# Norms of queries and keys by logarithm and exponential, and x centred and turned ahead of the bias layer's steps

## The reference

```python
xn = ln(x, g_norm)
q = (xn @ Wq).reshape(b, n, HEADS, DIM_HEAD).transpose(0, 2, 1, 3)
kv = xn @ Wkv
k, v = (kv[..., :DIM_HEAD], kv[..., DIM_HEAD:])
q = l2norm(q) * q_scale
k = l2norm(k) * k_scale
sim = jnp.einsum('bhid,bjd->bhij', q, k) * SCALE
bias = rel_pos_bias(n, w0, b0, g0, w1, b1, g1, w2, b2, q.dtype)
...
attn = jax.nn.softmax(sim, axis=-1)
out = jnp.einsum('bhij,bjd->bhid', attn, v)
...
def rel_pos_bias(n, w0, b0, g0, w1, b1, g1, w2, b2, dtype):
    pos = jnp.arange(-n + 1, n, dtype=dtype)[:, None]
    h = jax.nn.silu(ln(pos @ w0 + b0, g0))
    h = jax.nn.silu(ln(h @ w1 + b1, g1))
    h = h @ w2 + b2
```

## Time and profile before

| what | value |
|---|---|
| median of 3 runs (lowest to highest) | 252.21 us (251.5 to 252.31) |
| the profiled execution's own time | 251.66 us |
| its span | 249.9 us |
| busy: TensorE, VectorE, ScalarE, GpSimd | 210.8, 162.8, 122.1, 58.4 us |

### The profile page before, as it was taken

One profiled execution on the slowest core, in us unless ns is written; L12 is line 12 of the kernel. 1 busy time (PEld: TensorE's weight loads), 2 busy tenths in 40 slices (PEclk: granted clock), 3 DMA queues, 4 the chain that ended last, 5 costly groups with the idle time before them and its releaser, 6 DMA issues.

```text
span 249.9 us, 4768 instructions
## 1 busy us (share of the span) xinstructions
PE 210.8 (84%) x1906; PEld 141.4 (57%) x1906; DVE 162.8 (65%) x360; ACT 122.1 (49%) x178; POOL 58.4 (23%) x75
## 2 busy tenths in 40 slices
PE   0188798478897899999979989997889999999992
PEld 0154364343453464547356655764556899999992
DVE  2888779819148386889858975973953745474424
ACT  0216497677364255371634347538666542553230
POOL 3605949990000001200410027020003012000000
PEclk9999999999999999999999999999999999999997
DMA  6910055000003503400530070000000000000000
GB/s 187 422 44 0 0 146 199 4 1 0 3 0 63 129 3 107 84 0 3 116 77 0 24 155 16 0 3 0 3 3 1 4 0 21 3 21 0 21 0 21
DMA packets 10068, 11.75 MB, mean 47 GB/s; under 512 B 928, under 2 KB 9648, under 8 KB 9792
## 3 DMA queue, kind: packets, MB, share of 16 engines
q1 hardware_dynamic: 10048, 11.47, 16.5%
HBM read 10.38 MB, written 1.09 MB: 46 GB/s over the span
## 4 chain that ended last, share of the span: by engine, by line
PE 52%; DVE 27%; ACT 8%; POOL 5%; issue 4%; DMA 2%; DVEq 0%; SPq 0%; ACTq 0%
PE banks L1671 13%; PE banks L1376 6%; PE banks L1730 5%; DVE probs L958 5%; PE banks L1343 4%; PE banks L1271 3%; PE banks L1478 3%; PE banks L1396 2%; PE banks L1419 2%; PE banks L1438 2%; DMA rows<-in_rows 2%; ACT probs L594 2%; DVE zin L975 2%; ACT probs L556 2%; PE banks L1404 2%
## 5 line engine op out<-in xcount | busy, mean ns | idle before, releaser
L958 DVE TENSOR_TENSOR probs<-probs,eb 128x1024 f32<-128x1024 f32 x24 | 28.7, 1209 | 17.9 <-ACT probs L556 17.9
L594 ACT ACTIVATE probs<-banks,shift 128x1024 f32<-128x1024 f32 x24 | 25.9, 1112 | 14.9 <-PE banks L1461 14.7
L556 ACT ACTIVATE probs<-banks,key_shift 128x1024 f32<-128x1024 f32 x24 | 25.9, 1112 | 12.0 <-PE banks L1343 11.5
L1343 PE MATMUL banks<-qt,kT 64*128 64x512 f32 x96 | 25.4, 628 | 2.6 <-ACT probs L556 2.1
L1376 PE MATMUL banks<-probs,kvt 128*64 128x512 f32 (+1 forms) x128 | 23.3, 496 | 3.7 <-DVE probs L958 3.4
L363 POOL TENSOR_TENSOR qin<-qss,minus_half 128x16 f32<-128x16 f32 x8 | 23.1, 2903 | 6.4 <-DVE qss L797 6.3
L356 POOL TENSOR_TENSOR ve<-mv,ln_eps 128x2 f32<-128x2 f32 x4 | 1.7, 428 | 82.6 <-DVE mv L985 82.6
L1376 PEld LDWEIGHTS banks<-probs,kvt 128*64 128x64 f32 x128 | 7.8, 137 | 16.9 <-issue 9.7
L1671 PE MATMUL banks<-keys_space,wb 128*128 128x256 f32 (+1 forms) x72 | 17.3, 381 | 0.0
L1271 PE MATMUL banks<-wa,on 128*128 128x512 f32 x32 | 16.1, 628 | 1.2 <-DVE spread L803 1.2
L1203 DVE SCALAR_TENSOR_TENSOR x<-banks,ga,x 128x96 f32<-128x96 f32 (+1 forms) x32 | 10.2, 318 | 10.2 <-PE banks L1730 7.4
(11 more groups left out here) (214 smaller groups left out, 424.2 us busy)
## 6 DMA issues: line engine op xcount, KB each, us to landing
spread<-softmax_inverse_sums SPq DMA_DIRECT2D x16, 256.0 KB, 5.9
eb<-bias_table SPq DMA_DIRECT2D x4, 512.0 KB, 5.9
wb<-in_wb SPq DMA_DIRECT2D x1, 1842.0 KB, 10.5
wa<-in_wa SPq DMA_DIRECT2D x1, 1160.0 KB, 7.0
x<-in_x SPq DMA_DIRECT2D x1, 512.0 KB, 3.8
softmax_inverse_sums<-zin SPq DMA_DIRECT2D x4, 128.0 KB, 1.7
out<-x SPq DMA_DIRECT2D x4, 128.0 KB, 1.8
rows<-in_rows SPq DMA_DIRECT2D x1, 456.0 KB, 5.6
```

What stands on the lines that cost most here:

```text
L556: nc_.activation(pb[c], sc[:, 1024 * (c % 2):1024 * (c % 2 + 1)], ACT.Exp, bias=key_shift[:, b, k:k + 1]).then_inc(s["exp_done"], 1)
L594: nc_.activation(pb[c], sc[:, 1024 * SLOT[c]:1024 * (SLOT[c] + 1)], ACT.Exp, bias=shift2[:, 3:4]).then_inc(s["exp2_done"], 1)
L958: v.tensor_tensor(p, p, w, ALU.mult).then_inc(s["mult_done"], 1)
L1343: last = mm(out.rearrange("p (m i) -> p m i", m=rhs.shape[1]), lhs, rhs, start=True, stop=True)
```

## The change

- On ScalarE and GpSimd: the inverse roots of query tiles 3 to 7 and of the keys are no longer a power on GpSimd, or a square root on ScalarE with a reciprocal on VectorE, but exp(-0.5 ln) on ScalarE and one Newton step of four small instructions on GpSimd. Tiles 0 to 2 keep the power. The two loads of function tables in the stage are replaced by one, of a set that holds logarithm and exponential, between the last keys' copy and their turned copy.
- The keys are turned unscaled: GpSimd writes them twice side by side (`keys_doubled`), and their inverse length is applied as the scale of the exponentials of the first attention. `keys_out` moves from ScalarE to VectorE.
- The order at the end of the stage: two of the key turns go ahead of `turn_queries(5)`, two behind the first scores, which wait for the first sequence's keys alone; `queries_out(7)` stands behind the first exponential.
- In the front both halves of x have their statistics and the centring of the first half ahead of `bias_first`; the copies of the turned halves stand ahead of `bias_norm` and `bias_silu`; on TensorE keys and values of sequence 0 and queries 0 stand ahead of the turn of the bias rows and their product.

```diff
@@ gpsimd
+            def newton(ss, root, once, done):
+                def then(ins):
+                    steps[0] += 1
+                    ins.then_inc(s["root_step"], 1)
+                    pool.wait_ge(s["root_step"], steps[0])
+                then(pool.tensor_tensor(once, root, root, ALU.mult))
+                then(pool.tensor_tensor(once, once, ss, ALU.mult))
+                then(pool.tensor_scalar(once, once, -0.5, 1.5, ALU.mult, ALU.add))
+                pool.tensor_tensor(root, root, once, ALU.mult).then_inc(s[done], 1)
+            def query_newton(t):
+                pool.wait_ge(s["query_roots"], t - 2)
+                pool.wait_ge(s["qinv_ready"], t)
+                newton(qss[:, t], qin[:, t], q_once[:], "qinv_ready")
+            def key_newton():
+                pool.wait_ge(s["key_roots"], 1)
+                newton(kss[:], kin[:], ksr[:], "kinv_ready")
+            def keys_doubled():
+                pool.wait_ge(s["kvt_ready"], B)
+                pool.tensor_copy(kn, kvt[:].rearrange("p b t c -> p (b t) c")[:, :, None, 0:DH].to_broadcast([P, 3 * B, 2, DH])).then_inc(s["kn_ready"], 1)
...
             rstd(mv_x[:, 0:4, 1], ln_eps, ve_x[:, 0:4], rs_x[:, 0:4], s["x_stat"], s["x_rstd"], s["x_var"], 0)
+            rstd(mv_x[:, 4:8, 1], ln_eps, ve_x[:, 4:8], rs_x[:, 4:8], s["x_stat"], s["x_rstd"], s["x_var"], 1)
             rstd(bmv[:, :, 1], ln_eps, bve[:], brs[:], s["bias_var"], s["bias_rstd"], s["bias_pool"], 0)
-            rstd(mv_x[:, 4:8, 1], ln_eps, ve_x[:, 4:8], rs_x[:, 4:8], s["x_stat"], s["x_rstd"], s["x_var"], 1)
...
-            for t in range(5):
+            for t in range(3):
                 query_roots(t)
+            keys_doubled()
+            query_newton(3)
+            query_newton(4)
+            key_newton()
+            query_newton(5)
             later_windows(0)
-            query_roots(5)
+            query_newton(6)
             later_windows(1)
-            query_roots(6)
-            query_roots(7)
+            query_newton(7)
@@ scalar
             def key_roots():
-                nc_.preload_act_table(ACT.Sqrt)
                 act.wait_ge(s["kss_ready"], 1)
-                nc_.activation(ksr[:], kss[:], ACT.Sqrt).then_inc(s["ksr_ready"], 1)
+                nc_.activation(kin[:], kss[:], ACT.Ln).then_inc(s["key_logs"], 1)
+                act.wait_ge(s["key_logs"], 1)
+                nc_.activation(kin[:], kin[:], ACT.Exp, scale=-0.5).then_inc(s["key_roots"], 1)
+            def query_roots(t):
+                act.wait_ge(s["qss_ready"], t + 1)
+                nc_.activation(qin[:, t], qss[:, t], ACT.Ln).then_inc(s["query_logs"], 1)
+                act.wait_ge(s["query_logs"], t - 2)
+                nc_.activation(qin[:, t], qin[:, t], ACT.Exp, scale=-0.5).then_inc(s["query_roots"], 1)
...
             keys_values_raw(3)
+            nc_.preload_act_table_set("natural_log_exp_and_others")
             keys_values_tokens(3)
             bias_table()
             query_squares(3)
+            key_norms()
             queries_out(0)
-            key_norms()
+            query_roots(3)
             query_squares(4)
             queries_out(1)
+            query_roots(4)
+            query_squares(5)
             key_roots()
-            query_squares(5)
             queries_out(2)
-            nc_.preload_act_table_set("natural_log_exp_and_others")
+            query_roots(5)
             query_squares(6)
             queries_out(3)
+            query_roots(6)
             query_squares(7)
             queries_out(4)
             queries_out(5)
-            for b in range(B):
-                keys_out(b)
+            query_roots(7)
             queries_out(6)
-            queries_out(7)
             act.wait_ge(s["shifts"], 1)
+            act.wait_ge(s["kinv_ready"], 1)
...
-                               bias=key_shift[:, b, k:k + 1]).then_inc(s["exp_done"], 1)
+                               bias=key_shift[:, b, k:k + 1], scale=kin[:, b, k:k + 1]).then_inc(s["exp_done"], 1)
...
             weights(0, 0)
+            queries_out(7)
             weights(0, 1)
@@ vector
+            def keys_out(b):
+                dve.wait_ge(s["k_turned"], b + 1)
+                at = 512 * (b % 2)
+                v.tensor_scalar(kT[:, b], oa[:, at:at + 2 * P], qk_scale[:, 0:1], None, ALU.mult)
+                for e in range(2):
+                    r = slice(DH * e, DH * (e + 1))
+                    last = v.tensor_scalar(kx[r, b, e], oa[r, at + 2 * P:at + 2 * P + 2], qk_scale[r, 0:1], None, ALU.mult)
+                last.then_inc(s["kt_ready"], 1)
...
             x_stats(0)
-            bias_first()
             x_stats(1)
             x_centred(0)
-            bias_norm(0, R_G0)
+            bias_first()
             x_centred(1)
...
+            transposed(0)
+            bias_norm(0, R_G0)
+            transposed(1)
             bias_silu(0)
-            transposed(0)
             bias_transposed(0)
-            transposed(1)
             bias_second()
...
             queries_scaled(2)
-            key_sums()
             query_sums(4)
             queries_scaled(3)
+            key_sums()
             query_sums(5)
             queries_scaled(4)
-            keys_scaled()
             query_sums(6)
             queries_scaled(5)
+            queries_scaled(6)
             query_sums(7)
-            queries_scaled(6)
+            keys_out(0)
+            keys_out(1)
             queries_scaled(7)
+            keys_out(2)
+            keys_out(3)
@@ tensor
-            bias_turn(0)
...
             keys_values(0)
+            pe.wait_ge(s["xb_ready"], 2)
+            queries(0)
+            bias_turn(0)
+            turn_keys_values(0)
             pe.wait_ge(s["bias_hT"], 1)
...
-            pe.wait_ge(s["xb_ready"], 2)
-            queries(0)
-            turn_keys_values(0)
             queries(1)
...
             turn_queries(4)
+            turn_keys(0)
+            turn_keys(1)
             turn_queries(5)
-            for b in range(B):
-                turn_keys(b)
             turn_queries(6)
...
-            pe.wait_ge(s["kt_ready"], B)
+            pe.wait_ge(s["kt_ready"], 1)
             scores(0, 0)
+            turn_keys(2)
+            turn_keys(3)
             turn_queries(7)
```

More of the change, by code:

```diff
@@ L154, in adaln_ffn @@
         qin = sb("qin", [P, B * T, H])
+        q_once = sb("q_once", [P, H])
         qt = sb("qt", [P, B, M, S])
@@ L239, in adaln_ffn @@
             bias_top table_ready table_stored windows_loaded_0 windows_loaded_1 windows_copied bias_loaded
[L240 to L241 removed]
+            x_parts x_stat x_var x_rstd xc_ready xt_done xb_ready kv_proj kv_raw kv_turned kvt_ready ksq_ready kss_raw kss_ready key_logs key_roots kinv_ready kn_ready
+            query_logs query_roots root_step k_turned kt_ready q_proj qsq_ready qss_raw qss_ready qinv_ready qn_ready q_turned qt_ready
             qk_chunk qk_x exp_done px_exp px_ready mult_done pv_done z_done o_evac
@@ L366, in query_roots @@
                 inverse_roots(qss[:, t], qin[:, t], "qss_ready", t, "qinv_ready")
+            steps = [0]
+            def newton(ss, root, once, done):
[17 more added lines that the diff above has]
+                pool.tensor_copy(kn, kvt[:].rearrange("p b t c -> p (b t) c")[:, :, None, 0:DH].to_broadcast([P, 3 * B, 2, DH])).then_inc(s["kn_ready"], 1)
             def later_windows(g):
@@ L460, in key_roots @@
             def key_roots():
-                nc_.preload_act_table(ACT.Sqrt)
                 act.wait_ge(s["kss_ready"], 1)
-                nc_.activation(ksr[:], kss[:], ACT.Sqrt).then_inc(s["ksr_ready"], 1)
-            def keys_out(b):
-                act.wait_ge(s["k_turned"], b + 1)
-                at = 512 * (b % 2)
-                nc_.activation(kT[:, b], oa[:, at:at + 2 * P], ACT.Copy, scale=qk_scale[:, 0:1])
-                for e in range(2):
-                    r = slice(DH * e, DH * (e + 1))
-                    last = nc_.activation(kx[r, b, e], oa[r, at + 2 * P:at + 2 * P + 2], ACT.Copy, scale=qk_scale[r, 0:1])
-                last.then_inc(s["kt_ready"], 1)
+                nc_.activation(kin[:], kss[:], ACT.Ln).then_inc(s["key_logs"], 1)
[6 more added lines that the diff above has]
+                nc_.activation(qin[:, t], qin[:, t], ACT.Exp, scale=-0.5).then_inc(s["query_roots"], 1)
             def query_squares(t):
@@ L563, in extra_weights @@
                 nc_.activation(px[0:2], mb[0:2, 0:32].rearrange("p (e m q) -> p e m q", e=2, m=M), ACT.Exp,
-                               bias=key_shift[0:2, b, 2:3]).then_inc(s["px_exp"], 1)
+                               bias=key_shift[0:2, b, 2:3], scale=kin[0:2, b, 2:3]).then_inc(s["px_exp"], 1)
             def evacuate(b, g):
```

9 lines of the change are left out of this document (removed).

## The result

The changed kernel takes **253.76 us** (median of 5 runs, 253.26 to 254.77), the kernel before 251.76 beside it (5 runs): ratio 1.008, 95% interval 1.0056 to 1.0105. It is slower by some 2 us, where 1.1 us less was forecast, and it lies 0.26 us above the range. The first rival (a chance of 0.14, a price of 253.8) names what happened: TensorE's clock fell. That its price agrees with the measured time is partly luck, as the part on the prediction shows.

The account below looks back on a forecast made before the run. TensorE carries 52% of the chain of waits, VectorE 27%. Front and middle 0.0, tail -1.6, second pointer +0.5 sum to -1.1 us: 251.1 us against the median 252.21, range 249.3 to 253.5.

Parts of the forecast that it names:

- The first rival: Also rival 1: TensorE's clock falls in the new gap, about 24.3 to 27.2 us; +2.7, 253.8 us; chance 0.14.
- The front, x earlier: Start of the kernel: the last copy of x ends at 15.0 where it ended at 16.94, 1.9 us earlier.
- The bias layer later: Front: bias rows turn behind the first query product, clock rising near 18.1; first sums of squares 20.75 to 23.1, +2.35 us.
- To the first turn of queries: Delay carried on: fourth query product 29.41 to 31.1, +1.7 us; turn of queries 0 31.13 to 33.2, +2.05.
- The loop: Eight query tiles: tiles 3 to 7 save 1.25 us each; last scaling about 51.1 as now, so the middle sums to 0.0.
- rival 3: GpSimd's short steps stand still beside VectorE and late tiles slip: +2.3, 253.4 us; chance 0.05.
- The load: One table load between the last keys' copy and their turned copy: 1.28 us at about 30.9, next activation 0.02 us behind.
- rival 4: The table load costs a further wait as long as itself, 1.28 us: sum +0.2, 252.4 us; chance 0.05.
- The tail: End of the stage, reordered: third scores start at 54.9 where they started at 56.52, -1.6 us.
- rival 5: The tail's order yields nothing, as the last copy or bias rows' transfers come later: about +0.4, 252.6 us; chance 0.06.
- The second pointer: First attention's 28 exponentials get a per-partition scale, 0.1 us each; five in series in the chain: +0.5 us.
- Rival 2: TensorE's clock has risen by 15 us, so the first query product takes 1.9: 249.5 us; chance 0.10.

Follow-up runs that it names:

- kernel 1: Changed kernel with the front alone back in the old order on VectorE, GpSimd and TensorE: 249.53 us, ratio 0.989; measured once more 249.61, 0.9904.
- kernel 6: Changed kernel with the old front order, and query tiles 3 to 7 back to the power on GpSimd: 254.93 us, ratio 1.0119 to before.
- kernel 7: Changed kernel with the old front order, and the last copy of queries back ahead of the first exponential: 250.74 us, ratio 0.9976 to before.
- kernel 8: Changed kernel with the old front order, first attention's exponentials without the scale, so keys' lengths are left out: 248.98 us, ratio 0.9893 to before.
- kernel 2: Changed kernel with 12 idle TensorE products in the gap before the third keys' product: 252.1 us, ratio 1.0018 to the kernel before.
- kernel 3: Changed kernel with idle TensorE products in the gap and also in the front, up to the first query product: 250.36 us, ratio 0.9924 to before.
- kernel 9: Changed kernel with the old front order, plus 26 and 10 idle TensorE products before the turns of x: 248.31 us, ratio 0.9868 to before.
- kernel 10: Kernel before, with nothing of the change, plus 26 and 10 idle TensorE products before the turns of x: 250.99 us, ratio 0.998.
- kernel 11: Changed kernel with TensorE's old front order, plus 14, 4 and 14 idle products before x's turns and the bias rows' turn: 248.38 us, ratio 0.9884 to before.
- kernel 4: Kernel before with only the new order of the front; powers, square root, keys and tail as before: 258.12 us, ratio 1.0214.

## Why the prediction was wrong

**The front, x earlier: right.** The last copy of x ends at 15.0, as written. **The bias layer later: right in kind, too small.** It said +2.35 and was +3.40. The step that failed is "I take it that the rise stays at about 18.1". The product took 3.78 for 3.5, and behind it the bias rows' turn, the keys' turn and the bias product ran at half pace too (row L864 at 21.04, where 19.9 was forecast); the second query product still took 2.04. I had laid the rise at the moment of the trace before. There was only one execution to read it from, and that moment isn't a property of the kernel: the same list of TensorE up to the first query product gave 2.63, in kernel 1 3.74 and once more 3.20, in kernels 6, 7 and 8 3.01, 2.50 and 3.25. A trace records the granted clock only from its first rise on: that is 18.4 us before and 21.1 in the changed kernel, 3 us behind the 18.1 taken.

**To the first turn of queries: wrong, and the larger part of the miss.** +1.7 for the fourth query product was +5.0 (34.43 for 29.41), and +2.05 for the turn was +5.2. The step that failed is that the sum let TensorE go on at the full rate behind the new gap. Of the 3.3 us too many at the fourth product, 1.05 came with the front and 2.2 with the clock (34.43 for 32.25 in kernel 2). The latter is rival 1, and what was set against it did not bear on it: "the same stretch, with 1.44 us of work in 3.6, kept the full rate". That is an average over a stretch of the kernel before, whose longest gap there is 1.25 us. The forecast had itself a gap of 2.9 us from 24.3 to 27.2, for which the trace had no row. It came as 3.05, and the work behind it went to 1.2 GHz, until about 34.5. Experiment 2 shows cause and size at once: with work in the gap and no start moved, the middle is 2.0 us shorter. Rival 1's chance was too low, and its price of 253.8 met the measured 253.76 in part by luck: it had +2.7 for the clock, which cost 2.0, and nothing for the 1.05 of the front. It also had the loss in the wrong place: the fourth query product was to lose 1.7, but took 2.05 for 1.88, since the clock had risen by then; the keys' products and turns ahead of it were to lose 1.0 and lost 2.1.

**The loop: right.** With the clock kept, the middle gains 2.01 (kernel 2) where 2.35 was forecast. Kernel 2's first sums come 0.95 behind the forecast's 23.1; less that, its scalings of tiles 2 to 6 start within 0.1 us of the walk, the last one 0.3 behind it. Four Newton steps take 1.12 from 39.61 to the end of the last, with 1.1 forecast, so rival 3 is out. **The load: right.** 1.28 at 33.33, and the next copy 0.06 us behind its end, so rival 4 is out. **The tail: right**, -1.79 for -1.6; rival 5 is out. **The second pointer: right**, +0.50.

Put together: -1.1 as forecast, +1.05 in the front, +2.34 in the middle (2.0 of it the clock), -0.19 in the tail make the +2.1 of the spans. The mechanism by which the change was to earn held in every part; the sum failed on TensorE's clock, twice. Rival 2, the clock risen by 15, is what kernel 3's idle products bring about by hand.

What the sum also missed is a comparison it could have made. Moving the first query product ahead of the bias rows had no buyer: its result waits for VectorE, which is busy with what follows the bias rows. The prediction said that "nothing that came earlier is of use", and did not ask which engine's list was to blame. Kernel 5, the change with these lines of TensorE left in the old order, is 1.5% faster than the change. The change's small loss is thus two effects of opposite sign: 2.4 to 2.8 us earned, 4.4 to 4.8 lost.

## What to carry to other kernels

A step that moves a late branch later must be followed to the gap that it opens on TensorE, and the gap can have a second price, the half rate of what comes behind it for some us; an average of busy time over a stretch with shorter gaps is no evidence that a longer one is safe. When two branches start on one engine, ask which has the longer tail of small dependent steps: here it had to go first, even though the other was ready. A few idle products, where the engine has nothing to do and nothing waits behind them, bought 1.6 us in kernel 2 and a further 2.4 in kernel 3; in kernels 9, 10 and 11 it was 0.5 to 1.0, hardly clear of nothing by the intervals.

## What was not expected of the hardware

**The rise of the clock varies from execution to execution**, and by as much as the smaller edits here are worth: the first query product took from 2.50 to 3.74 us behind the same instructions, and 1.88 to 1.99 with idle products ahead. In all of them the granted clock reads 1.00 there. At half pace this is no reading: the trace has no record of the clock ahead of its first rise, and the profile shows 1.00 for that. The first record starts between 18.4 and 21.5 us in the ten executions without idle products in the front, and between 6.9 and 8.6 in the four with them; ahead of it, only durations show the half rate. The Trainium skill says the same of the start: TensorE: Matmul & The Clock Gate (What's actually happening) has the number of slow first products vary between runs of one kernel.

**The clock falls in the middle of the kernel.** It fell behind gaps of 3.05, 3.15 and 2.04 us (the changed kernel, kernels 4 and 6), and held behind 1.25, 0.66 and even 1.88 us. That last one is in the kernel before, whose turn then takes 1.09:

```profile
46.38 1.09 PE L1281 MATMUL banks<-ident,spread 128*128 128x128 f32 x8 [1.88 <-DVE spread L803]
```

The length of a gap alone isn't shown to decide: in 3 of the kernel before's 71 executions beside the experiments the mean granted clock is 0.981 to 0.989, and they took 252.48 to 254.32 us.

**A transfer set the old front's start.** VectorE waits for `rows` in it, for up to 1.97 us. Kernels 1 and 7:

```profile
7.42 0.61 DVE L858 SCALAR_TENSOR_TENSOR scratch<-rows,pos 128x128 f32<-128x128 f32 x2 [1.51 <-DMA rows<-in_rows]
```
```profile
7.84 0.61 DVE L858 SCALAR_TENSOR_TENSOR scratch<-rows,pos 128x128 f32<-128x128 f32 x2 [1.97 <-DMA rows<-in_rows]
```

In kernel 9 the same instruction starts at 6.13 without a wait. In the four kernels with idle products in the front (3, 9, 10, 11) the transfer took 4.7 to 5.0 us from issue to landing, in all others 5.4 to 6.5; why is open, and so is how much of what idle products bought in kernels 9 and 10 is this. The new order of VectorE never waits there, since x comes first; with TensorE's order old, this gained nothing that the times show.
